# Gathering one tile of every second attention batch by single-row DMAs from SyncE instead of by GpSimd's indirect DMA

## The reference

```python
h = relu(layernorm(x))
# layer 0, attention with 4 heads of 32
h = (h @ W.T).reshape(N, 4, 32)
alpha = leaky_relu((h * att_src).sum(-1)[src] + (h * att_dst).sum(-1)[dst], 0.2)
ex = exp(alpha - segment_max(alpha, dst)[dst])
w = ex / segment_sum(ex, dst)[dst]
x = x + segment_sum(h[src] * w, dst) + bias
# layer 1, a two-layer network on every edge
h = relu(layernorm(x))
m = relu(concat(h[src], h[dst], edge_attr) @ W1 + b1) @ W2 + b2
x = x + segment_sum(m, src)
```

## Time and profile before

| | |
|---|---|
| median of 3 runs | 5701.07 us (5699.46 to 5702.33) |
| the profiled execution | 5682.86 us, span 5681.1 us |
| busy share of the span | PE 90%, PEld 72%, DVE 69%, ACT 52%, POOL 68% |
| granted TensorE clock, mean | 0.936 of full speed |
| DMA | 995.58 MB, mean 175 GB/s |

### The profile page before, as it was taken

One profiled execution on the slowest core, in us unless ns is written; L12 is line 12 of the kernel. 1 busy time (PEld: TensorE's weight loads), 2 busy tenths in 40 slices (PEclk: granted clock), 3 DMA queues, 4 the chain that ended last, 5 costly groups with the idle time before them and its releaser, 6 DMA issues.

```text
span 5681.1 us, 160364 instructions
## 1 busy us (share of the span) xinstructions
PE 5111.3 (90%) x34188; PEld 4074.0 (72%) x34189; DVE 3923.1 (69%) x14222; ACT 2971.1 (52%) x8485; POOL 3871.0 (68%) x3713
## 2 busy tenths in 40 slices
PE   4888888888888886999999999999997999999999
PEld 3777777777777774677666666666665888887788
DVE  6777877878778776555455555555455888888887
ACT  3566666666666653333333333332223777777776
POOL 4777777777777774677777777777776555555553
PEclk7889889889889987999999999999998999999999
DMA  4522222222222234999888988888886999999997
GB/s 109 165 54 54 54 54 54 54 54 54 54 54 54 54 105 139 278 275 270 262 263 258 266 262 260 262 264 259 262 257 186 224 221 222 222 221 217 217 222 193
DMA packets 860128, 995.58 MB, mean 175 GB/s; under 512 B 307993, under 2 KB 663225, under 8 KB 859776
## 3 DMA queue, kind: packets, MB, share of 16 engines
q1 hardware_dynamic: 662496, 610.19, 39.9%
q0 software_dynamic: 190592, 379.87, 24.6%
q10 hardware_dynamic: 6816, 3.38, 0.2%
HBM read 728.41 MB, written 264.62 MB: 175 GB/s over the span
## 4 chain that ended last, share of the span: by engine, by line
PE 59%; DMA 9%; issue 9%; DVE 9%; POOL 8%; DVEq 3%; ACT 3%; POOLq 0%; ACTq 0%; SPq 0%
PE bank L1703 12%; PE bank L1536 12%; PE bank L1626 8%; PE bank L1628 7%; PE bank L1693 7%; DMA xr<-arena 6%; POOL xr L547 5%; PE bank L1457 3%; POOL arena L499 2%; DVE arena L945 2%; DVEq L251 2%; DVE arena L1048 2%; PE bank L1616 1%; DMA arena<-xr 1%; DVE arena L1028 1%
## 5 line engine op out<-in xcount | busy, mean ns | idle before, releaser
L499 POOL DMA_INDIRECT arena<-h_tab,arena x1612 | 1557.1, 966 | 543.0 <-issue 420.7
L547 POOL DMA_INDIRECT xr<-arena x1612 | 1568.5, 973 | 511.7 <-issue 352.6
L1536 PE MATMUL bank<-arena 128*128 128x136 f32 x6448 | 1311.0, 332 | 78.3 <-DVE arena L1048 11.0
L719 ACT ACTIVATE arena<-bank 128x256 f32<-128x256 f32 x1612 | 591.3, 384 | 1389.6 <-PE bank L1628 932.0
L1626 PE MATMUL bank<-arena 128*128 128x256 f32 x3224 | 1023.4, 400 | 91.8 <-DVE arena L1244 45.1
L1536 PEld LDWEIGHTS bank<-arena 128*128 128x128 f32 x6448 | 980.9, 214 | 162.6 <-DVE arena L1048 67.0
L561 POOL DMA_INDIRECT arena<-p_tab,arena x428 | 671.3, 1569 | 622.3 <-DMA arena<-p_tab,arena 498.4
L626 ACT ACTIVATE arena<-bank 128x256 bf16<-128x256 bf16 x1612 | 614.7, 381 | 792.8 <-PE bank L1457 708.6
L1628 PE MATMUL bank<-arena 128*128 128x256 f32 x3224 | 971.3, 383 | 0.0
L1703 PE MATMUL bank<-arena 128*128 128x257 f32 x3424 | 901.5, 386 | 6.3 <-issue 2.6
L1048 DVE TENSOR_TENSOR arena<-arena,bank 128x272 f32 x1612 | 693.6, 430 | 212.7 <-PE bank L1536 186.0
(11 more groups left out here) (260 smaller groups left out, 6595.3 us busy)
## 6 DMA issues: line engine op xcount, KB each, us to landing
arena<-xr SPq DMA_DIRECT2D x428, 520.0 KB
arena<-q_tab SPq DMA_DIRECT2D x1612, 128.0 KB
arena<-in_edge_attr SPq DMA_DIRECT2D x61, 832.0 KB
arena<-rel_tab SPq DMA_DIRECT2D x124, 224.0 KB
arena<-h_tab,arena POOLq DMA_INDIRECT x1612
xr<-arena POOLq DMA_INDIRECT x1612
arena<-rel_tab SPq DMA_DIRECT2D x124, 192.0 KB
xr<-arena SPq DMA_DIRECT2D x26, 520.0 KB
```

The costliest lines, as they stand in the source:

```text
L499: pool.indirect_dma_start(G[:, q, t, :], None, h_tab, bass.IndirectOffsetOnAxis(ap=idx[:, q, t:t + 1], axis=0)).then_inc(sem(f"gath{q}"), 16)
L547: pool.indirect_dma_start(xr, bass.IndirectOffsetOnAxis(ap=pos[:, q, t:t + 1], axis=0), Rb[:, t, :], None).then_inc(sem(f"scat{m}"), 16)
L1536: last = pe.matmul(PSB[3 + t % 2][:, k * H * MW:(k + 1) * H * MW], OH[:, (t + 2 * q) % 4, k * P:(k + 1) * P], flat(msg[:, t, :, :]), start ...
```

## The change

SP gathers tile 0 of every odd batch from batch 3 on (30 tiles), by 128 DMAs of one row each, into a staging tile `stage` of 128 rows. The 128 row numbers come first, by a DMA from `src` into one partition (`srow`), and then by four register loads of 32 values. ACT copies the finished tile into `G[:, 1, 0, :]`, at t = 20 of the odd batch two before the one that uses it. POOL leaves these 30 gathers out. The copy tells two readers by `stage_free`: SP, which may then fill `stage` for the next odd batch, and DVE, whose `"logits"` step waits for it beside the gathers.

SP's new loop stands in its list ahead of the node loads and of all writes into `xr`. The semaphores `x_in0` to `x_in3` and `xr_in0` to `xr_in3` are merged into `slot_in0` to `slot_in3`, and the counts of `gath1` are made smaller; both leave the order of the work as it is.

```diff
+            def gather_rows(i):
+                sp.wait_ge(sem("stage_free"), i)
+                sp.dma_start(srow, src[bass.ds((2 * i + 1) * (BT * P), P)].rearrange("(a n) -> a n", a=1)).then_inc(sem("srow_in"), 16)
+                sp.wait_ge(sem("srow_in"), 16 * i)
+                sp.nop(nofuse=True)
+                for half in range(2):
+                    for g in range(2):
+                        e0 = half * (P // 2) + g * (P // 4)
+                        regs = nc.values_load_multi_w_load_instructions(
+                            srow[0:1, e0:e0 + P // 4], engines=[ENG.SP], min_val=0, max_val=N - 1,
+                            skip_runtime_bounds_check_because="the source node of an edge")[1]
+                        for e in range(P // 4):
+                            sp.dma_start(stage[e0 + e:e0 + e + 1, :], h_tab[bass.ds(regs[e], 1), :]).then_inc(sem(f"stage_in{half}"), 16)
             sp.wait_ge(sem("hx_used"), NCH)
+            with sp.Fori(1, NB // 2) as i:
+                gather_rows(i)
             sp.wait_ge(sem("msg_ready"), 4)
             load_nodes(0)
...
                     for t in range(h * (BT // 2), (h + 1) * (BT // 2)):
+                        if q == 1 and t == 0 and not first:
+                            continue
...
+            pool.wait_ge(sem("hx_used"), NCH)
+            M.memset(stage, 0.0).then_inc(sem("stage_free"), 1)
             gather(0, 0, True)
...
+            def staged(b, i):
+                act.wait_ge(sem("msg_ready"), 4 * b + 1)
+                for half in range(2):
+                    act.wait_ge(sem(f"stage_in{half}"), 16 * (P // 2) * (i + 1))
+                A.activation(G[:, 1, 0, :], stage, ACT.Copy).then_inc(sem("stage_free"), 1)
...
                     if ahead1 and t == 19:
                         chain_exp(b + 1)
+                    if q == 1 and ahead2 and t == 20:
+                        staged(b, i)
...
-                    dve.wait_ge(sem(f"gath{q}"), 16 * BT * (i + 1))
+                    dve.wait_ge(sem(f"gath{q}"), 16 * (BT - q) * i + 16 * BT)
+                    if q == 1 and not (isinstance(i, int) and i == 0):
+                        dve.wait_ge(sem("stage_free"), i + 1)
```

More of the change, by code:

```diff
@@ L52 @@
 RW = HID + 4
-GSUM = 16 * BT * (NB // 2)
+GSUM = (16 * BT * (NB // 2), 16 * (BT + (BT - 1) * (NB // 2 - 1)))
 PM = 7
@@ L131, in gnn @@
         sgn, below, halves = X([TP], BF16), X([2, NB + 2]), X([NB + 2])
-        X([6500 - 264 - 1664 - 56 + 1664 - 824 - 128 - 64])
+        stage, srow = X([GW]), X([P], I32, 1)
+        X([6500 - 264 - 1664 - 56 + 1664 - 824 - 128 - 64 - 136 - 128])
         idx = X([2, BT], I32)
@@ L265, in _ @@
             for c in range(NCH - 1):
-                sp.dma_start(xs[:, c * NC:(c + 1) * NC, :], rows(x, c)).then_inc(sem(f"x_in{c}"), 16)
+                sp.dma_start(xs[:, c * NC:(c + 1) * NC, :], rows(x, c)).then_inc(sem(f"slot_in{c}" if c < NS else f"x_in{c}"), 16)
             r0 = (NCH - 1) * NC * P
@@ L427, in load_xr @@
                     sp.wait_ge(sem("hid_ready"), c * CP - (NS - 1) * CP)
-                sp.dma_start(XR[:, s, :, :], xr[bass.ds(c * (CP * GR), CP * GR), :].rearrange("(k p j) w -> p k (j w)", p=P, j=PR)).then_inc(sem(f"xr_in{s}"), 16)
+                sp.dma_start(XR[:, s, :, :], xr[bass.ds(c * (CP * GR), CP * GR), :].rearrange("(k p j) w -> p k (j w)", p=P, j=PR)).then_inc(sem(f"slot_in{s}"), 16)
             for s in range(NS):
@@ L557, in source_add @@
                 pool.wait_ge(sem("idx_ready"), NB + NS * i + s + 1)
-                pool.wait_ge(sem(f"gath{s % 2}"), GSUM + 16 * len(NADD[s]) * n)
+                pool.wait_ge(sem(f"gath{s % 2}"), GSUM[s % 2] + 16 * len(NADD[s]) * n)
                 pool.nop(nofuse=True)
@@ L673, in _, with batch @@
                 turn_out(1, 1, t)
-            def batch(b, q, ahead2=True, ahead1=True, first=False):
+            def staged(b, i):
[3 more added lines that the diff above has]
+                A.activation(G[:, 1, 0, :], stage, ACT.Copy).then_inc(sem("stage_free"), 1)
+            def batch(b, q, ahead2=True, ahead1=True, first=False, i=None):
                 widen(b, q, 0, first)
@@ L697, in batch @@
                         chain_exp(b + 1)
+                    if q == 1 and ahead2 and t == 20:
+                        staged(b, i)
             batch(0, 0, first=True)
-            batch(1, 1)
+            batch(1, 1, i=0)
             with nc.Fori(1, NB // 2 - 1, engines=[ENG.Activation], head_slot={ENG.Activation: 0}) as i:
                 for q in range(2):
-                    batch(2 * i + q, q)
+                    batch(2 * i + q, q, i=i)
             batch(NB - 2, 0, ahead2=False)
@@ L794, in relu @@
                 if added(s, k):
-                    act.wait_ge(sem(f"gath{s % 2}"), GSUM + 16 * len(NADD[s]) * (c + 1))
+                    act.wait_ge(sem(f"gath{s % 2}"), GSUM[s % 2] + 16 * len(NADD[s]) * (c + 1))
                 A.activation(hid[:, m % 2, :, 0:HID], XR[:, s, k, :].rearrange("p (j w) -> p j w", j=PR)[:, :, 0:HID], ACT.Relu).then_inc(sem("hid_ready"), 1)
@@ L835, in centred @@
                 v, m = xs[:, c * NC:(c + 1) * NC, :], mean[:, c * NC:(c + 1) * NC]
-                dve.wait_ge(sem(f"x_in{c}"), 16 + (32 if c == NCH - 1 else 0))
+                dve.wait_ge(sem(f"slot_in{c}" if c < NS else f"x_in{c}"), 16 + (32 if c == NCH - 1 else 0))
                 link(V.tensor_reduce(m, v, AX.X, ALU.add))
@@ L1339, in hotp @@
                 if k == 0:
-                    dve.wait_ge(sem(f"xr_in{s}"), 16 * (i + 1))
+                    dve.wait_ge(sem(f"slot_in{s}"), 16 * (i + 2))
                     n = len(NADD[s])
```

## The result

The changed kernel takes 5736.88 us (median of 4 runs, 5733.54 to 5748.69) against 5700.26 in the same comparison: **1.0069 times as long, 95% interval 1.0052 to 1.0086**. A second comparison, beside the experiments, gave 1.0079 (1.0065 to 1.0093). So it is slower by 37 to 44 us, where +280 was forecast, and far under the range.

What follows compares the result with a forecast made beforehand. POOL was taken to pace the attention stage at 65.97 us a pair, other engines nearly as slow. SP's loop, +239, and late writes into xr, +41, made +280 on 5701.07, rounded to 5980 us; range 5800 to 6250.

Steps and rivals of the forecast that it cites:

- What bounds the kernel: Attention stage: POOL's gathers, 1.26 us each, pace a pair of batches at 65.97 us, other engines nearly as slow.
- the gain: 30 gathers off POOL, 37.7 us, counted as no more than DVE's 21.2 us of waits for gathers.
- A loop through SP sets the pair: Attention stage: SP refills staging after ACT's copy, ACT copies after all rows land; the pair lasts the longer of 65 and L.
- L: One turn of SP's staging loop, from copy to copy: 74.2 us (68.2 to 90.6).
- +239: Loss in us from SP's loop over 29 turns, 29 x (74.2 - 65.97); bounds +65 to +714.
- The row DMAs: 128 one-row DMAs in SP's loop, 0.45 us a row: 57.6 us (54.3 to 66.9).
- The register loads: Four register loads of 32 values in SP's loop: 12 us (10.2 to 15.8).
- The row numbers: DMA of 128 integers from DRAM in SP's loop, with register work: 2.2 us (1.8 to 3.7).
- Landing and copy: Last row's landing, 1.7 us, and ACT's copy with two semaphores, 0.7, in SP's loop: 2.4 us.
- lower bounds: Low ends of two steps in SP's loop: 54.3 us for 128 row DMAs, 10.2 for four register loads.
- The late writes: Writes into xr move behind SP's loop, so DVE's denominators wait at the attention stage's end: +41 us.
- Rival 1: SP's loop is hidden, about 62 us a turn, but writes into xr are late: net +17, 5718 us; chance 0.05.

Runs made afterwards that it cites:

- the even relief: The kernel before, with POOL leaving out the first tile of every even batch from batch 2 on, zeros copied instead: 0.9955, -25 us.
- The run with the writes first: The change, with node loads and 26 writes into xr behind SP's first loop turn, not its last: 1.0015 against the kernel before, +8.5 us.
- the halves version: Against the kernel before: shortened SP loop staging even batches' first tile, copied in two halves, writes into xr one a turn: 1.0039.

## Why the prediction was wrong

- **What bounds the kernel: POOL paces it only in part, and the gain was read too coarsely.** A gather less is 1.26 us of POOL, and the pair fell from 65.97 by 0.29 us only. The waits for gathers were read as one sum. Batch by batch they are mostly the even batches', and the change relieves the odd ones: -10 us instead of -21. Nor were these waits the most that could be won: the even relief won 25 us and took away only 12 us of them.
- **A loop through SP sets the pair: right.** The chain of waits is SP's, ACT waits at t = 20, and a turn longer by 1.33 us costs 29 times that.
- **"L = 2.2 + 12 + 57.6 + 2.4 = 74.2 us": the step that failed.** The mechanism was right and the size off. The turn is 66.5 us, and since only the 0.5 to 0.7 us above 65.97 count, 8 us too many in L made +239 out of about +20. The terms:
  - *The row DMAs*, 57.6 (54.3 to 66.9): the issue is 0.225 us, and in the chain the rows follow each other in 0.408 (1000.10, 1000.51, 1000.91 ...), so 52.2 for 128. My lower bound used the median of one line, 0.234, and 0.19 of register work; its own row had a minimum of 0.215. That is 5.4 us.
  - *The register loads*, 12 (10.2 to 15.8): four took 2.05 + 2.12 + 2.12 + 2.27 = 8.6. I drew a line through 4 values and 26 beyond its end; 32 values took hardly longer here than the 2.10 us of 26 there. And I went 1.8 us up towards SP's own 3.21, for loads behind DMAs; here they stayed between 2.04 and 2.30. On a line through 16 values (1.23) and 32 (2.12), 26 would take 1.8; why they took 2.1 stays open. The term is 3.4 us too large.
  - *The row numbers*, 2.2: 1.3 to 1.5 and the register work.
  - *Landing and copy*, 2.4: about 2.0, from the last issue at 1072.7 to 1074.75. But they lie beside a stall that I did not have at all, the branch's, which lasts until 1075.3. Such steps without a term gave back some of the 8.8 us by which rows and loads were too large, so that L was 7.7 too long.
  - Both "lower bounds" were estimates with a point of their own, and both lay above the truth. Where a term is compared with 65.97, an L of 66 to 74 had to be held open.
- **The late writes: right.** +41 forecast; 35.1, 33.9 and 31.3 us of gap in three traces, and +31 us when they alone are late. The stage ended 58.0 us after the copy in batch 59, where 57.7 was forecast, and the node stage, which waits for the writes, began 93.1 after it, where 99 was. Rival 1 put this beside a hidden loop, at 5718; that the changed kernel lies there plus the loop's 20 us is partly luck, since a relief of 10 instead of 21 us and a gap shorter than 38 offset each other.
- **The sum** as the runs have it: relief -10, late writes +31, and the rest of 37 to 44, some 16 to 23, for a turn that is longer than the pair. The run with the writes first gives 18.5 for it by itself.
- The Trainium skill, page Runtime: NRT & Kernel Launch, section Instruction fetch mechanics, says of a register load some 200 ns a register. Here it is 0.066 us, 2.12 for 32, loaded from an on-chip tile, so for such loads the measurement decides. The same section says that a taken branch to a target outside the instruction window forces a fetch before execution goes on. The 2.4 to 3.1 us behind SP's branch are consistent with that. The traces count instruction packets as well: 335 in the changed kernel, 279 with its loop written out, 187 before, and two of them in the halves version's gap from 1043.2 to 1046.4. Whose they are, and whether SP waited for them, no run shows.

## What to carry to other kernels

Where work is moved to an idle engine's queue, write its list out as a loop, from the moment a buffer comes free to the moment it is free again, and compare that turn with the pace it has to meet: below the pace it costs nothing, above it every fraction of a microsecond counts once a turn, and a forecast has to keep both sides open when the terms don't settle which it is. Look at what stood behind the new work in that queue, because it now comes when the new work ends. And look at which instances of a wait are real before thinning out the work behind it: 30 gathers were worth 10 us in one half of the batches and 25 in the other.

## What the runs showed of the hardware that was not expected

- A DMA of one row from SP, with its address from a register, costs 0.408 us from start to start (0.225 of issue); 3,840 of them beside POOL's gathers did not measurably slow the stage, as long as a turn was shorter than the pair (0.9983 with them, 0.9982 without, each to within 0.0009).
- A taken branch at the end of a loop body of some 400 instructions left SP idle for 2.4 us (1072.90 in the changed kernel) to 3.1 us (1043.2 to 1046.3 in the halves version). Written out, with constant addresses, the list ran without the gap, and, each against the kernel before in its own comparison, the change became 19 to 26 us faster and the halves version some 46.
- Register loads: 1.23 us for 16 values, 2.12 for 32.
